# Where ScalarE writes the logits and the normalised rows: at the end of a step, or in the step behind it

## The reference

```
scores = einsum('bgqsd,bgtd->bgqst', qb, kb) * scale   # causal
ao     = einsum('bgqst,bgtd->bgqsd', softmax(scores), vb)
h1     = hidden_states + einsum('sbh,oh->sbo', ao, proj_weight)
ln2    = layer_norm(h1) ;  logits = ln2 @ router_weight
top_p, top_i = top_k(softmax(logits), 2)      # rows go to their experts
out    = h1 + sum over both experts of  p * (gelu(ln2 @ w1) @ w2)
```

## Time and profile before

| | us |
|---|---|
| median of three runs | 1193.75 (1191.47 to 1196.36) |
| the profiled execution | 1190.08 |
| its span in the trace | 1188.3 |
| TensorE busy in the span | 1094.4 (92%) |
| VectorE | 920.2 (77%) |
| ScalarE | 811.3 (68%) |
| GpSimd | 549.9 (46%) |

### The profile page before, as it was taken

One profiled execution on the slowest core, in us unless ns is written; L12 is line 12 of the kernel. 1 busy time (PEld: TensorE's weight loads), 2 busy tenths in 40 slices (PEclk: granted clock), 3 DMA queues, 4 the chain that ended last, 5 costly groups with the idle time before them and its releaser, 6 DMA issues. The chain is left out here.

```text
span 1188.3 us, 24750 instructions
## 1 busy us (share of the span) xinstructions
PE 1094.4 (92%) x8034; PEld 996.9 (84%) x8036; DVE 920.2 (77%) x2290; ACT 811.3 (68%) x1840; POOL 549.9 (46%) x504
## 2 busy tenths in 40 slices
PE   7899999999999888988889898899999999999993
PEld 4799999999999677777777776789999889989983
DVE  6677777777777579899999877986877777777771
ACT  2466676676675578888888778657676667776770
POOL 0022222212212233477877766687854455554556
PEclk9999999999999989999999998999999999999997
DMA  8422533533422113345544466678777677676754
GB/s 301 112 97 93 157 107 112 168 100 121 137 76 94 55 44 92 98 141 148 158 142 137 140 200 209 158 187 213 183 195 186 160 181 199 175 172 173 188 126 46
DMA packets 119016, 171.79 MB, mean 145 GB/s; under 512 B 14508, under 2 KB 90188, under 8 KB 118860
## 3 DMA queue, kind: packets, MB, share of 16 engines
q1 hardware_dynamic: 92300, 136.00, 37.0%
q0 software_dynamic: 26592, 34.24, 15.1%
HBM read 104.04 MB, written 67.97 MB: 145 GB/s over the span
## 5 line engine op out<-in xcount | busy, mean ns | idle before, releaser
L1438 POOL DMA_INDIRECT out_rows<-y,row x142 | 237.7, 1674 | 173.3 <-DVE y L2042 79.9
L1973 DVE TENSOR_TENSOR hl<-h,hh 128x512 fp32r<-128x512 f32 (+1 forms) x156 | 99.4, 642 | 81.7 <-ACT h L1644 78.5
L179 PE MATMUL gh<-w2h,hh 128*128 128x256 f32 x568 | 160.7, 283 | 1.1 <-issue 1.1
L181 PE MATMUL gh<-w2h,hl 128*128 128x256 f32 x568 | 160.8, 283 | 0.0
L180 PE MATMUL gh<-w2l,hh 128*128 128x256 f32 x568 | 160.7, 283 | 0.0
L1643 ACT ACTIVATE hh<-gw 128x512 fp32r<-128x512 f32 (+1 forms) x78 | 44.1, 565 | 127.8 <-issue 126.2
L1416 POOL DMA_INDIRECT slot_rows<-kept,slot x104 | 110.4, 1062 | 28.7 <-issue 28.4
L179 PEld LDWEIGHTS gh<-w2h,hh 128*128 128x128 f32 x568 | 108.9, 192 | 2.4 <-issue 1.2
L180 PEld LDWEIGHTS gh<-w2l,hh 128*128 128x128 f32 x568 | 108.9, 192 | 1.2
L181 PEld LDWEIGHTS gh<-w2h,hl 128*128 128x128 f32 x568 | 108.9, 192 | 0.0
L934 POOL TENSOR_TENSOR layer_low<-whole,layer_high 128x528 fp32r<-128x528 f32 x32 | 41.7, 1324 | 140.8 <-ACT layer_high L854 140.8
(11 more groups left out here) (374 smaller groups left out, 3892.2 us busy)
## 6 DMA issues: line engine op xcount, KB each, us to landing
w1e<-in_moe_w SPq DMA_DIRECT2D x39, 512.0 KB, 5.8
w2e<-in_moe_w SPq DMA_DIRECT2D x39, 512.0 KB, 3.5
xr<-slot_rows SPq DMA_DIRECT2D x32, 532.0 KB, 5.4
xg<-x_rows SPq DMA_DIRECT2D x62, 260.0 KB, 3.2
x_rows<-x SPq DMA_DIRECT2D x32, 264.0 KB, 2.9
xT<-in_xT SPq DMA_DIRECT2D x32, 256.0 KB, 2.7
x<-in_x SPq DMA_DIRECT2D x32, 256.0 KB, 3.4
x_rows<-whole SPq DMA_DIRECT2D x32, 256.0 KB, 2.5
```

The lines of the kernel that those rows point to most:

```text
L179: nc.tensor.matmul(out, at_a(ah), at_b(bh), start=first, stop=False, skip_group_check=True)
L181: return nc.tensor.matmul(out, at_a(al), at_b(bh), start=False, stop=last, skip_group_check=True)
L1438: g.indirect_dma_start(out=out, out_offset=bass.IndirectOffsetOnAxis(ap=row[m % NR][:, t:t + 1], axis=0), in_=y[m % 2][:, t, :], in_offset ...
L1973: v.tensor_tensor(hl[m % 2][:, f, 0:n], h[:, f, 0:n], hh[m % 2][:, f, 0:n].bitcast(F32), ALU.subtract).then_inc(hl_did, 1)
```

## The change

The block with the four instructions goes from the end of ACT's step to a place behind the first exponentials, and works there on the pair of one step further back, `k - 3` in place of `k - 2`. Nothing is added or removed.

```
                 exponentials(0)
+                if has(k - 3):
+                    for u in places:
+                        after(act, dve_did["shift"], k - 3, U2 - 1)
+                        a.activation(pr.logits[:, group(k - 3, u), :], h1[u][:, D:WIDE], ACT.Copy,
+                                     scale=rstd[:, u:u + 1]).then_inc(act_did["logit"], 1)
+                        a.activation(pr.rows[:, group(k - 3, u), 0:D], h1[u][:, 0:D], ACT.Identity,
+                                     scale=rstd[:, u:u + 1], bias=shift[:, u:u + 1]).then_inc(act_did["nrm"], 1)
                 if has(k + 1):
                     heads(k + 1, 0)
...
                 for m in chosen_at(k - 1):
                     take_ranks(m)
-                if has(k - 2):
-                    for u in places:
-                        after(act, dve_did["shift"], k - 2, U2 - 1)
-                        a.activation(pr.logits[:, group(k - 2, u), :], ...
-                        a.activation(pr.rows[:, group(k - 2, u), 0:D], ...
```

## The result

| | before | after |
|---|---|---|
| median | 1193.47 us (1191.47 to 1196.36) | 1243.76 us (1236.78 to 1252.48, 4 runs) |
| the profiled execution | 1190.08 | 1252.48 |
| its span | 1188.3 | 1250.7 |

The ratio of after to before is 1.0423, 95% interval 1.0353 to 1.0493: slower, by 50.3 us between the medians. The forecast was 1240 us (1226 to 1256).

The account below looks back on a forecast made before the run. A chain through ACT, PE and DVE was taken to set the loop's pace. 1190.08 + 34.15 (insertion) + 10.9 (clock falls) + 2.5 (loop end) = 1237.6 us, or 1241.3 from the median; forecast 1240 us, range 1226 to 1256.

Parts of the forecast that it names:

- Nothing gained ahead of the exponentials: Removing the block before ACT's first exponentials gains 0 of 1.40 us a step, since DVE's difference hides it.
- 1.40 us per turn: Block between ACT's first exponentials and `pwT` lengthens each of 28 turns, steps 3 to 31: 39.2 us.
- DVE's lateness: In 12 late turns DVE starts its maximum later than PE's scores allow; this absorbs 5.05 us, leaving 34.15.
- the two rings: Pacing chain of the loop: ACT exponentials and `pwT`, PE product and scores, DVE maximum and difference; 8.67 us a turn.
- The falls: PE's longer wait for `pwT` drops its clock in 10 of 28 turns, 8 more than before: 10.9 us.
- the third rival: PE's clock falls in every turn, 26 further falls at 1.66 us: 1269.9 or 1274 us; chance 0.07.
- My reason for so few: Slow products on PE fill its next wait, making two falls in a row less likely; hence 10 of 28.
- The end of the loop: Pair 30's logits and rows come behind the four passes of `features(0)`, delaying the first expert block: 2.5 us.
- the sum: Profiled execution 1190.08 plus 34.15 for the insertion, 10.9 for the clock, 2.5 after the last step: 1237.6 us.
- The first: Rival: no further fall of PE's clock in the loop, 1226.7 or 1230 us; chance 0.13.
- the second: Rival: DVE, late by over 1.40 us each turn, hides the insertion; 1192.6 or 1196 us, no change; chance 0.04.
- the fourth: Rival: ACT held the exponentials, so their earlier start shortens turns by up to 1.40 us; 1150.9 us; chance 0.02.

## Why the prediction was right

The mechanism is the predicted one, and it is shown, not only argued: the same four instructions one step later cost nothing that could be told ahead of the exponentials, and half of them behind cost 0.98 us a step.

- **Nothing gained ahead of the exponentials.** Right: ACT now idles there for 2.12 us (predicted 2.1), until DVE's difference ends.
- **1.40 us per turn.** Measured 1.36 in the timeline and 10.04 - 8.67 = 1.37 per plain step; from exponentials to product 461.48 - 457.06 = 4.42 us (predicted 4.46). Less DVE's lateness I had 34.15 us; the two rings without falls differ by 34.79. Of that lateness the 1.57 us of step 28 were the idle `h` of that execution: with the block ahead of the exponentials, and with the idle products, the same step takes 8.67.
- **The falls.** Predicted 10 in the 28 turns at 1.36 us, 10.9 more than before. There were 12 at 1.34, and by the four rings 12.16 us more, by the turns that hold them 13.4. The two prices behind the mean, 1.66 and 1.06, came back as 1.63 and 0.94, in six turns of each kind (the first with a chosen batch cost 2.19). That only 12 of 28 waits led to a fall is against the third rival. My reason for so few did not hold: falls came in two turns running only once (703.18 and 715.75 us), but not because slow products shorten the next wait: behind the products of 492.50 it is 1.96 us as ever. So it is in part luck that 10 stands so near 12. Its upper bound, two in three, rested on three of the seven long waits of before; the other four, 1.66 to 1.83 us, had led to none. The prediction also took one wait, 1.99 us, for every turn; the six with a chosen batch came to wait 2.85 us and more, and all of them fell, while of the others only 6 in 22 did. By the Trainium skill, "TensorE: Matmul & The Clock Gate", section "A second HAM failure mode: psum-queue depth-cycling", which describes another kernel, short idle spells of PE make the clock swing and the throughput is lost in the swings; the idle products bear this out for this loop, 308.69 to 292.57 us, though not for every spell.
- **The end of the loop.** 2.28 us (predicted 2.5). With the block ahead of the exponentials 0.93 of it stayed, the place behind the four passes; the other 1.35 are the insertion in step 31, where exponentials to product take 3.55 us and took 2.20 before.
- **What was not in the sum.** The ring came out 1.9 us longer than predicted (46.95 against 45.05). The steps up to 3 were put down at nothing, as the block is not yet in them; the clock stayed low there for 13 us, and they took 3.11 more. Other executions show 23.59 us (with half the block, and with the block behind `pwT`), so this is at least in part the run. The opening's 7.74 us are the run alone (below). With these three and the 2.32 of the rest, less 0.22 at the end of the loop, the 1237.6 of the sum becomes the 1252.48 of the profiled execution; between the medians, 50.3 us stand against 47.5.
- **The rivals.** The first fell with the 12 falls, the second with DVE's 29 waits for the scores, the fourth with ACT's 26 waits for DVE: DVE hides no more of the insertion than what falls into its own lateness, 34.79 us being left of 28 times 1.37.

## What to carry to other kernels

When engines pass work round in a ring, ask of each instruction whether it stands on the ring's path or beside it: the same 1.4 us cost nothing beside DVE's maximum and difference, and 1.24 us per turn (34.79 over 28) on the path, although ScalarE, which runs them, was busy for only 68% of the span and 82% of this stage. Then ask what the longer wait does to TensorE: its clock added a third of that price or a little more. And a place late in a step is not free either, if what it reads is overwritten early in the next one.

## What the runs showed of the hardware

Products that compute nothing made kernels faster: the one before by 0.45%, with an interval that just excludes no change, the changed one by 22 to 24 us. They fill PE's wait and the granted clock stays at 1.00; without them it fell, in the changed kernel, at every wait of 2.85 us or more and at 6 of 22 of 1.95, in a steady pattern: from 492 to 683 us at every second wait. With half the block, slow products followed no wait of 1.57 us and three of the seven of 2.47 to 2.65.

The opening, the same code in every kernel here, took from 407.86 to 421.78 us in the profiled executions, and the clock goes with it. Its first 405 us in the changed kernel:

```profile
0.00:405.00 405.00, 387.21 (x3040) 369.30 (x3042) 291.61 (x744) 248.32 (x584) 75.51 (x100) 0.97 0.41 123
```

In the kernel before with idle products, whose opening took 409.23 us:

```profile
0.00:405.00 405.00, 387.80 (x3097) 368.35 (x3099) 295.24 (x750) 253.88 (x594) 76.60 (x101) 0.99 0.41 126
```

The profiled executions with the longest opening, 419.39 and 421.78 us, are also the slowest of their kernels, 8.7 and 11.3 us above the medians. In both the clock stood at its lower level for 27.3 us of the opening, in the other seven for 4.1 to 14.2. What decides in which runs it falls there stays open.
